# A kernel of two transformer blocks: VectorE's dependent pairs as separate steps, and the order of every engine laid anew

## The reference, cut to what matters

```python
def attn_layer(x, Wqkv, qs, ksc, Wo):                  # x: 8 x 256 x 128
    q, k, v = split(x @ Wqkv)                          # 16 heads of 64 each
    q = l2norm(q) * qs; k = l2norm(k) * ksc
    q = q*cos*scale + rotate_half(q)*sin*scale         # k with 1/scale
    out = local_attention(q, k, v)                     # windows of 32, looks one window back
    return out @ Wo
def ffn_layer(x, g, bln, W1, b1, W2, b2):
    xn = layernorm(x) * g + bln
    a, gate = split(xn @ W1 + b1)
    return a * gelu(gate) @ W2 + b2
# six times: x = x + attn_layer(shift_tokens(x)); x = x + ffn_layer(shift_tokens(x))
```

## Time and profile before

| | us |
|---|---|
| median of 3 runs | 1952.4 (1951.92 to 1953.56) |
| profiled execution, span | 1955.3 |
| PE busy | 1866.8 (95%) |
| ACT busy | 1592.8 (81%) |
| DVE busy | 1587.6 (81%) |
| POOL busy | 1069.6 (55%) |

### The profile page before, as it was taken

How to read it: one execution, slowest core, us unless ns; L and a number is a source line. 1 busy time by engine, 2 the same in 40 slices (tenths; PEclk the granted TensorE clock), 3 DMA queues, 4 the chain that set the end, 5 groups by cost and what they waited for, 6 DMA issues and landing times.

```text
span 1955.3 us, 77164 instructions
## 1 busy us (share of the span) xinstructions
PE 1866.8 (95%) x34029; PEld 1568.0 (80%) x34029; DVE 1587.6 (81%) x2234; ACT 1592.8 (81%) x2751; POOL 1069.6 (55%) x523
## 2 busy tenths in 40 slices
PE   6899999878999999999999999999999999999987
PEld 4788989856878888888878888887888888888876
DVE  3566765478898988989888998988898998989873
ACT  2578878667988888898988889897888889888864
POOL 3333222176565666657566666756575666657530
PEclk7999999979999999999999999999999999999998
DMA  6333322023335343353434443444434344333341
GB/s 175 121 127 124 105 80 66 2 72 96 105 99 156 96 132 111 105 150 95 124 100 130 123 125 108 112 122 122 113 103 132 97 137 129 105 115 94 101 105 29
DMA packets 134183, 212.35 MB, mean 109 GB/s; under 512 B 26871, under 2 KB 51034, under 8 KB 133850
## 3 DMA queue, kind: packets, MB, share of 16 engines
q1 hardware_dynamic: 133676, 207.36, 37.0%
q10 hardware_dynamic: 174, 0.05, 0.0%
HBM read 136.76 MB, written 70.60 MB: 106 GB/s over the span
## 4 chain that ended last, share of the span: by engine, by line
PE 86%; ACT 6%; DVE 5%; issue 3%; DMA 0%; ACTq 0%; SPq 0%; DVEq 0%
PE o_pair L799 9%; PE bank L747 9%; PE bank L882 9%; PE s_pair L769 7%; PE bank L724 7%; PE bank L725 6%; PE bank L726 6%; PE bank L781 4%; PE bank L649 4%; PE bank L904 3%; PE bank L816 2%; PE bank L817 2%; PE bank L818 2%; PE bank L887 2%; PE s_pair L760 1%
## 5 line engine op out<-in xcount | busy, mean ns | idle before, releaser
L1734 POOL TENSOR_TENSOR rt<-raw,rot 128x1024 f32<-128x1024 f32 x192 | 456.3, 2377 | 353.5 <-PE bank L747 328.8
L1743 POOL TENSOR_TENSOR rt<-rt,t 128x2048 f32<-128x2048 f32 x96 | 439.5, 4578 | 178.7 <-DVE t L1541 175.1
L724 PE MATMUL bank<-wqkv,xs 128*128 128x512 f32 x576 | 257.4, 447 | 11.6 <-ACT vn L1080 6.7
L1063 ACT ACTIVATE raw<-bank 128x512 f32<-128x512 f32 x384 | 223.2, 593 | 28.2 <-PE bank L726 14.9
L1528 DVE TENSOR_REDUCE bank<-t 128x32 f32<-128x2048 f32 x96 | 219.7, 2289 | 17.1 <-ACT t L1071 12.6
L726 PE MATMUL bank<-wqkv,xs 128*128 128x512 f32 x576 | 229.9, 399 | 0.0
L725 PE MATMUL bank<-wqkv,xs 128*128 128x512 f32 x576 | 229.8, 399 | 0.0
L747 PE MATMUL bank<-const,rt 128*128 128x128 f32 x1536 | 219.8, 281 | 9.5 <-issue 3.2
L799 PEld LDWEIGHTS o_pair<-pT,v 64*64 64x64 f32 x12288 | 196.2, 135 | 40.3 <-ACT oT L1119 17.6
L1541 DVE TENSOR_TENSOR t<-raw,bank 128x1024 f32<-128x1024 f32 x192 | 225.0, 1213 | 0.6
L1549 DVE TENSOR_TENSOR rt<-rt,bank 128x2048 f32<-128x2048 f32 x96 | 219.6, 2288 | 3.3
(11 more groups left out here) (403 smaller groups left out, 4157.5 us busy)
## 6 DMA issues: line engine op xcount, KB each, us to landing
v<-v_rows SPq DMA_DIRECT2D x288, 256.0 KB, 4.4
v_rows<-vn SPq DMA_DIRECT2D x192, 256.0 KB, 3.7
v<-v_rows SPq DMA_DIRECT2D x96, 192.0 KB, 3.2
w_parts<-wqkv SPq DMA_DIRECT2D x30, 512.0 KB, 3.8
wqkv<-w_parts SPq DMA_DIRECT2D x30, 512.0 KB, 4.1
wraw<-in_L_ffn_Wqkv_dram SPq DMA_DIRECT2D x36, 256.0 KB, 3.1
w_parts<-wqkv SPq DMA_DIRECT2D x10, 341.0 KB, 3.7
w<-w_parts SPq DMA_DIRECT2D x10, 341.0 KB, 5.7
```

What stands on the lines that cost most here:

```text
L724: pe.matmul(bank[:, :], hi, w[:, 0, :], start=True, stop=False)
L1063: act.activation(k.raw_r[c][:, n * 512:(n + 1) * 512], k.one.at["qk", j][:, :], ACT.Copy)\
L1734: e = pool.tensor_tensor(heads(k.rt_r[c][:, part]), heads(k.raw_r[c][:, part]), cosv, ALU.mult)
L1743: pool.tensor_tensor(k.rt_r[c][:, :], k.rt_r[c][:, :], k.t2[:, :], ALU.add).then_inc(s["rot_add"], 1)
```

## The change

First, the class `Own` gets `mark` (add to the own semaphore and remember the count under a name) and `after` (wait for that count). On DVE the dependent pairs of `late` become steps of their own, with a slot each: `ss | ssf`, `rnp | nrm`, `top | sub`, `sum | rec | div`, `hn_mul | hn_hi | hn_lo`. The instructions are the same; a semaphore's wait now stands ahead of the second of a pair, in its own slot. `top` waits for `smax` of the same chunk's unit before where it waited for `pe_pT` and `ssum`; `sub` has the wait on `pe_pT`; `sum` waits for the earlier `rec`, and `rec` for the earlier `ssum`.

```diff
+    def mark(self, instruction, name, v):
+        self.n += 1
+        instruction.then_inc(self.sem, 1)
+        self.at[name, v] = self.n
+
+    def after(self, name, v):
+        self.engine.wait_ge(self.sem, self.at[name, v])
...
-            settle(dve.tensor_reduce(head_rows(sm[:, 2, :]), p, AX.X, ALU.add))
-            settle(dve.reciprocal(k.rec_p[c], sm[:, 2, :]))
+            if u:
+                after("rec", 2 * u + c - 2)
+            mark(dve.tensor_reduce(head_rows(sm[:, 2, :]), p, AX.X, ALU.add), "sum", 2 * u + c)
+
+        def invert_sum(c):
+            after("sum", 2 * u + c)
+            if u:
+                dve.wait_ge(s["ssum"], 2 * u + c - 1)
+            mark(dve.reciprocal(k.rec_p[c], k.sm_r[c][:, 2, :]), "rec", 2 * u + c)
+
+        def divide(c):
+            p = k.p_r[c][:, :, :, :].rearrange("p h r j -> p r h j")
+            after("rec", 2 * u + c)
             dve.tensor_tensor(p, p, head_rows(k.rec_p[c]).unsqueeze(3).to_broadcast([P, 2, HP, 2 * WIN]), ALU.mult)\
                 .then_inc(s["ssum"], 1)
...
+        yield from t.to("sum0")
         softmax_sum(0)
...
+        yield from t.to("rec0")
+        invert_sum(0)
+        yield from t.to("div0")
+        divide(0)
```

Second, every table is laid anew, in slots an eighth as long:

```diff
-ATTENTION_START, ATTENTION_SPACING = 6, 40
-EXPERTS_START, EXPERTS_SPACING = 70, 40
-LATE_START, LATE_SPACING = 376, 32
+ATTENTION_START, ATTENTION_SPACING = 48, 320
+EXPERTS_START, EXPERTS_SPACING = 560, 320
+LATE_START, LATE_SPACING = 3008, 256
...
-PE_AT = dict(qk00=30, qk01=30, qk02=30, qk03=30, qk10=38, qk11=41, qk12=45, qk13=47, v00=58, v01=62, v10=63, v11=65,
+PE_AT = dict(qk00=658, qk01=679, qk02=742, qk03=742, qk10=811, qk11=872, qk12=873, qk13=884, v00=937, v01=947, v10=981,
```

129 lines of the change are left out of this document (80 added, 49 removed).

## The result

| | before, us | after, us |
|---|---|---|
| median of 4 runs | 1952.2 (1950.7 to 1953.6) | 2174.7 (2170.2 to 2183.1) |
| ratio, with its 95% interval | 1 | 1.113 (1.109 to 1.117) |
| profiled execution, span | 1955.3 | 2168.8 |
| L0's wo | 475.12 | 522.35 |
| 45 intervals of wo, L0 to L45 | 1412.85 | 1578.21 |

What follows compares the result with a forecast made beforehand. PE, busy 95% of the span, was taken as the bound. 1955.3 - 4 + 10 + 4 + 0 - 1 = 1964.3 us profiled, about 1961 as median (profiled run 2.9 above it); 8-in-10 range 1944 to 1974.

Steps and rivals of the forecast that it cites:

- The late units stay at their floor: Late units: PE, busy 31.0 of 31.0 us in a steady unit, leaves each at its floor, 30.73 us.
- forecast (a): Whole kernel: E7's chain is exposed and late units stay at their floor; 1961 us, range 1957 to 1968, chance 0.43.
- (d): Rival, late units: var or v11 comes 0.3 us late every unit, on top of the forecast; 1975 us, chance 0.14.
- the sign of being wrong that I gave for the late units: The prediction is wrong if late units take clearly less than 45 x 31.4 us.
- The early phase keeps its order and so its time (0, -3 to +3): Early phase, ahead of the late units: order unchanged, so 0 us, bounds -3 and +3.
- Part 2: Transition: late work begins behind E7's steps, so E7's chain is exposed; +10 us, bounds 0 and +16.
- E7: Experts ahead of the late units; its chain of LayerNorm, scores, threshold, attend was to leave PE 14 us of gap.
- the rotation begins 0.6 us behind the last of the four products: Transition: L0's rotation on POOL starts at 402.8 us, 16.2 later than before.
- the replay: Transition: E7's chain and L0's fill recomputed with durations of before; L0 begins near 399.4, its wo at about 485 us.
- Part 1: DVE in late units: six pairs set apart save 0.12 us each, 0.7 a unit; -4 us, bounds -24 and +14.
- Part 3: SP's order at the five changes of layer: pair01 may come late for a00; 0.8 us each, +4, bounds 0 and +13.
- Part 4: Late units: var close behind mean keeps 0.3 us of slack; 0 us, or +14 if late by 0.3 a unit.

Runs made afterwards that it cites:

- experiment 6: The kernel of experiment 2 with the early-phase tables (attention and experts, all engines) of the kernel before, times eight; 2040.3 us, 24.6 below experiment 2.
- experiment 8: The kernel of Experiment 1 with LATE_START 3424, late work 52 old slots later, behind E7's steps; 1985.1 us, ratio 1.0145.
- experiment 9: The kernel of experiment 8 with DVE making L0's cosine table ahead of its first sum of squares; 1975.2 us, ratio 1.009.
- Experiment 1: The changed kernel's code with the old tables times eight, both halves of a pair in one slot, so the order of before; 1954.8 us, ratio 0.9995.
- experiment 2: The changed kernel with seven PE steps moved, so up, transposes and products stand between scores and attends; 2064.9 us, ratio 1.056.
- experiment 11: The old order with PE's v01 between a10 and a11, and ACT's copy of it ahead of the copy of o; 1960.1 us, ratio 1.002.
- experiment 5: The kernel before with two extra DRAM-to-DRAM transfers of 512 KB in every late unit; 1974.8 us, ratio 1.010.

## Why the prediction was wrong, step by step

- **"The late units stay at their floor"** (forecast (a), and "for it: PE at 31.0 of 31.0") is the step that failed, and 165 of the 213.5 us hang on it. The floor was right, even 0.3 us too high: a unit without a gap takes 30.46. Only 3 of the 45 intervals are at it, though; their mean is 35.1. I asked of the new order on PE only whether each step's data are there in time, and not how fast PE eats its instructions. The sign was in the trace: "6.0 us are six gaps at the scores in which nothing the profile shows was waited for". I set them aside as a constant, and misread the view besides: it has 14.2 us without a name, and I took one line of four. They were what I had no cause for, and that cause is what grew, to 125 us; with the slow work at the lower clock behind many of the gaps it is all of the 165. A fixed distance between such gaps, 61 x 253.5 instructions, could have been counted in the windows view ahead of the prediction.
- None of the rivals had it. (d), the dearest, had 1975. The range of 1944 to 1974 was made of bounds on named waits only, and the sign of being wrong that I gave for the late units looked for less than 45 x 31.4 us alone.
- **"The early phase keeps its order and so its time (0, -3 to +3)"** failed: +24 (experiment 6), bound +3. The new order was in the tables for all to see; I compared the transition and the steady part and not this one.
- **Part 2**, E7's chain exposed: the mechanism is right (experiment 8, the end to a us, with two errors inside that cancel), and in the changed kernel the transition costs 23.4 us. The term was mis-sized: +10 taken, upper bound +16, and alone it costs L0 21 us and the time 30. What failed is "the rotation begins 0.6 us behind the last of the four products": it also needs `rot`. Before, DVE made it at 384.82, just in time for 386.57, and POOL's wait named `xT`; I took the named one for the only one. With E7 out of the way the table was the last to come: 411 for 402.8. By experiment 9 that is 5 of the 21 us. Two more things the replay lacked: behind the gaps of E7's chain PE runs at the lower clock (0.78 us for a product of 0.48), and PE waits 8 to 11 us for `xs`, which POOL does behind rotation and addition.
- **Part 1**: the price of 0.12 us a pair is right, its effect on the time is not shown. Experiment 1 keeps the pairs together and shows only that the steps cost nothing; and (rows below) L1577 takes 1.25 us from start to start where its L1585 stands behind it, and 1.13 where an instruction of another unit does. DVE's busy time fell by 15 us; the 34 were meant start to start. The -4 that I took for the two waits for DVE can't be seen beside the gaps.

```profile
1366.72 1.22 DVE L1577 TENSOR_REDUCE sm<-s_pair 128x16 f32<-128x1024 f32 x1
1367.97 1.22 DVE L1585 TENSOR_TENSOR p<-s_pair,sm 128x1024 f32<-128x1024 f32 x1
...
1386.57 1.22 DVE L1577 TENSOR_REDUCE sm<-s_pair 128x16 f32<-128x1024 f32 x1
1387.70 0.48 DVE L1612 SCALAR_TENSOR_TENSOR hh<-bank,cols,hh 128x256 f32<-128x256 f32 x1
```

- **Part 3**: +4 taken; four waits of the attend for `v<-v_rows`, 3.9 us in all, longest 1.7. Right in size and place as to these waits. But the five intervals in which a layer changes take 40.4 us in the mean and the other forty 34.4 (before: 32.8 and 31.2): the three longest fetch gaps, 3.8, 3.9 and 4.1 us, stand in them. Unnamed gaps take 5.3 us in each of the five and 2.5 in each of the others, so the DMAs that meet there cost PE more through its instructions than through v.
- **Part 4**: var waits for nothing in the changed kernel between the first and the last of the 45 intervals, so 0 was right. How little room there is shows in experiment 2, where one product moved ahead of the attends and PE waited 0.66 us for `hn` in 41 units.

## What to carry to other kernels

Where a kernel has runs of very short instructions on one engine (here a matmul or a weight load takes 6 to 8 ns of the run), the order sets how fast the instruction stream is eaten; spread the short ones among long ones before asking anything of waits. A gap that no semaphore explains is to be counted in instructions: if such gaps lie whole multiples of one number apart, it is fetch, and a shift of the program by some instructions proves it. Count the semaphore instructions with the rest. Look also at what data the DMA engines carry when such a run stands on the engine. And where PE's clock falls behind a gap, the gap costs more than itself: in the changed kernel 125 us of unnamed gaps came with 70 us of slow work; in the one before, 14 us with about 3, since most of its gaps left the clock alone.

## What the runs showed of the hardware

- PE's instructions come in packets of 16.4 KB, 256 instructions, through a DMA queue of their own. The packet for the next block mostly starts when PE has entered the block ahead, 0.9 us (before) and 1.2 us (after) behind that in the median; from the entry to the first instruction of the new block it took 4.5 us in the example, with the DMA engines at 0.86 up to the packet; 1.1 of it is the packet, and 1.2 to 1.6 come behind it. The Trainium skill, "Runtime: NRT & Kernel Launch", section "Instruction fetch mechanics", has the blocks of 16 KiB or 256 instructions, fetched by the sequencer's own DMA queue one ahead; the trace agrees, with packets of 16.4 KB, gaps at whole multiples of 256 instructions, and one packet for each block. It says that crossing a block's edge is "mostly hidden"; here 124.9 us in the late units of the changed kernel are not. It also gives PE a store of 2048 instructions; no packet here comes early enough to show such a store in use, and one short block alone was enough for a stall.
- The lower clock follows idle times of PE as short as 1.2 us, though not each: 0.61 and 0.54 in the four us behind the gap of 2.43; behind the one at 1355.56, of 1.19, the next products took 0.78 and 0.63 us; behind the one at 1323.55, of 1.12, the stretch up to the next gap kept 1.00. Its length alone does not decide: the gaps of 2.58 us at 552.35 and 2.16 at 620.28 left the clock at 1.00 for the next four us, as did the one of 2.25 at 1737.60 in the kernel before.
- A dependent pair on DVE costs 0.12 us more from start to start than an independent one (1.25 and 1.13). The Trainium skill, "VectorE: DVE Perf Modes", section "The DRAIN you can't avoid", has a semaphore behind each of eight copies cost nothing over one behind the last. No run here tests that: the 0.12 us are for an instruction that waits for the one ahead of it, and experiment 1 adds steps on an engine that doesn't bound the kernel.
- A change from one kind of matmul to another costs PE about 0.3 us, in both directions together (experiment 11: 30.73 to 31.06 for the shortest full interval, with one run of attend split in two).
- What stays open: how far ahead PE's fetch looks, why about one packet in ten starts before PE's entry into the block ahead, and why with the DMA engines over 0.8 busy the packet's start lies 2.6 us behind the entry in the changed kernel and 1.6 in the one before. Busy DMA engines are part of it (experiment 5); no run separated the rest.
